# Two cross-attention layers on one core: inputs handed over transposed, x projected in float32, new instruction orders

## The reference

```python
# layer 0
q = x @ Wq + bq; k = ctx @ Wk + bk; v = ctx @ Wv + bv
w = softmax(q @ k.T / 16, axis=queries)        # over the 512 rows of x
x = layernorm(w @ v + x) * gamma + beta
# layer 1
Q = x @ Wq1 + bq1; K = ctx @ Wk1 + bk1; V = ctx @ Wv1 + bv1
out = x + (softmax(Q @ K.T / 16, axis=keys) @ V) @ Wo + bo
```

## Time and profile before

| | us |
|---|---|
| Median of 3 runs (467.13 to 467.44) | 467.43 |
| The profiled execution | 466.4 |
| Its span, first to last instruction | 464.6 |
| Border: `project_q1(0)` starts | 60.4 |
| Borders: `project_q1(1)` to `project_q1(7)` start | 113.7, 167.0, 220.2, 273.6, 327.0, 379.3, 428.2 |

### The profile page before, as it was taken

The page is one execution under the profiler, slowest core; times in us unless marked ns, Lnnn a source line. Parts: engine busy times, 40 slices in busy tenths (PEclk is TensorE's granted clock), DMA queues, the critical chain, the costliest instruction groups (busy, mean ns, idle before and its releaser), DMA issues.

```text
span 464.6 us, 7967 instructions
## 1 busy us (share of the span) xinstructions
PE 443.7 (96%) x2433; PEld 371.6 (80%) x2433; DVE 366.8 (79%) x898; ACT 383.7 (83%) x819; POOL 365.0 (79%) x321
## 2 busy tenths in 40 slices
PE   8798899999999999999999999999999999799796
PEld 8686667887888888888888878888888878687596
DVE  3798978788886988778787888779877887578774
ACT  4899889987999789987899879987899879872473
POOL 0567699979999799887999789987999699963400
PEclk9999999999999999999999999999999999999999
DMA  9400200021100210020200210001100010000001
GB/s 262 130 24 24 71 24 2 23 72 34 36 23 1 72 47 23 24 55 18 70 23 1 71 49 23 24 18 55 46 1 0 3 46 1 0 0 25 23 1 45
DMA packets 23896, 17.29 MB, mean 37 GB/s; under 512 B 1055, under 2 KB 23854, under 8 KB 23854
## 3 DMA queue, kind: packets, MB, share of 16 engines
q1 hardware_dynamic: 23706, 16.66, 11.8%
q10 hardware_dynamic: 148, 0.13, 0.1%
HBM read 12.59 MB, written 4.19 MB: 36 GB/s over the span
## 4 chain that ended last, share of the span: by engine, by line
PE 79%; ACT 8%; DVE 5%; POOL 4%; issue 4%; DVEq 0%; POOLq 0%; ACTq 0%
PE ps_l L654 11%; PE ps_l L655 10%; PE ps_l L656 9%; PE ps_s L800 9%; PE ps_s L654 8%; PE ps_s L656 8%; PE ps_s L655 8%; ACT p L1048 3%; PE ps_s L774 3%; PE ps_s L841 3%; DVE max L1257 2%; POOL wsum L1376 2%; PE ps_l L687 2%; ACT p L1001 2%; PE ps_s L768 2%
## 5 line engine op out<-in xcount | busy, mean ns | idle before, releaser
L1376 POOL TENSOR_TENSOR wsum<-wsum,p 128x512 f32<-128x512 f32 (+1 forms) x88 | 116.3, 1322 | 13.4 <-ACT p L1007 11.8
L1383 POOL TENSOR_TENSOR p_lo<-p,p_hi 128x512 fp32r<-128x512 f32 (+1 forms) x91 | 117.2, 1295 | 2.6 <-ACT p_hi L1015 2.4
L1001 ACT ACTIVATE p<-s_sb,min 128x512 f32<-128x512 f32 (+1 forms) x104 | 75.4, 726 | 7.5 <-DVE min L1171 5.3
L1171 DVE CUSTOM_DVE_ANT_0 s_sb<-ps_l,cb 128x512 f32<-128x512 f32 (+1 forms) x104 | 70.4, 685 | 13.3 <-ACT p L1001 5.5
L1007 ACT ACTIVATE p<-p,r 128x512 f32<-128x512 f32 (+1 forms) x104 | 74.9, 728 | 1.4 <-DVE r L1178 1.3
L1192 DVE TENSOR_TENSOR p1T_lo<-ps_s,p1T_hi 128x512 fp32r<-128x512 f32 (+1 forms) x91 | 60.6, 683 | 14.4 <-ACT p1T_hi L1056 13.9
L1257 DVE TENSOR_REDUCE max<-ps_s 128x1 f32<-128x804 f32 x58 | 57.1, 992 | 10.0 <-PE ps_s L656 8.6
L1056 ACT CAST p1T_hi<-ps_s 128x512 fp32r<-128x512 f32 (+1 forms) x91 | 52.0, 586 | 14.9 <-PE ps_s L800 12.1
L1015 ACT CAST p_hi<-p 128x512 fp32r<-128x512 f32 (+1 forms) x104 | 63.5, 624 | 0.5 <-PE ps_l L656 0.4
L1048 ACT ACTIVATE p<-ps_s,bias 128x1206 f32<-128x1206 f32 (+1 forms) x58 | 53.6, 927 | 3.6 <-DVE bias L1268 3.1
L800 PE MATMUL ps_s<-ident,p 128*128 128x128 f32 (+1 forms) x364 | 49.6, 273 | 1.5 <-ACT p L1048 1.5
(11 more groups left out here) (181 smaller groups left out, 1100.1 us busy)
## 6 DMA issues: line engine op xcount, KB each, us to landing
ctx_sb<-in_ctx_dram SPq DMA_DIRECT2D x24, 256.0 KB, 2.9
x_sb<-in_x_dram SPq DMA_DIRECT2D x8, 512.0 KB, 3.6
out_dram<-y_res SPq DMA_DIRECT2D x16, 256.0 KB, 2.2
p<-in_L_xattn_Wq_dram SPq DMA_DIRECT2D x2, 256.0 KB, 4.2
ctx_sb<-in_ctx_dram SPq DMA_DIRECT2D x8, 32.5 KB
p<-in_L_xattn_Wv_dram SPq DMA_DIRECT2D x2, 128.0 KB, 4.3
p<-in_L_xattn_Wo_dram SPq DMA_DIRECT2D x1, 256.0 KB, 4.7
p<-in_L_xattn_Wk_dram ACTq DMA_DIRECT2D x1, 128.0 KB, 3.3
```

The costliest lines, as they stand in the source:

```text
L1001: nc.scalar.activation(p0[0:m, ring0(i), :], s0_sb[0:m, (a + i) % 2, :], ACT.Exp, bias=min0[0:m, i:i + 1], scale=-1.0, accum_out=sum0[0:m, ...
L1171: nc.vector.tensor_tensor_reduce(out=s0_sb[0:m, (a + i) % 2, :], in0=ps_s0[0:m, (a + i) % 2, :], in1=cb[a % 2][0:m, :], scale=-SCALE, scal ...
L1376: nc.gpsimd.tensor_tensor(total, total, p0[0:m, ring0(i), :], ALU.add).then_inc(wsum_done, 1)
L1383: nc.gpsimd.tensor_tensor(p0_lo[0:m, h, :], p0[0:m, ring0(i), :], p0_hi[0:m, h, :].bitcast(F32), ALU.subtract).then_inc(p0_lo_done, 1)
```

## The change

The host now hands over x and ctx both as they are and transposed, and the weights transposed; bias vectors come as columns. So `turn_x`, `turn_ctx`, `turn_wq`, `turn_wk`, `turn_vectors`, `turn_w1`, `x_turned`, `xT_low` and `repeat` are gone. `project_q0` takes the transposed x directly in two plain float32 products. `ctx_high` and `ctxT_low` read the loaded `ctxT_sb` in SBUF. ctx has one buffer, ctxT one, xT two. In batch 0 the context is split on GpSimd (`ctx_split_first`) and the odd tiles' `p0_high` on VectorE (`p0_high_first`). `residual1` is two instructions. SP's order and all four engines' orders are new.

```diff
         x_sb = [sb(f"x_sb{p}", [P, TB, E]) for p in range(2)]
-        ctx_sb = [sb(f"ctx_sb{p}", [P, MT, L]) for p in range(2)]
+        xT_sb = [sb(f"xT_sb{p}", [P, EC, T]) for p in range(2)]
+        ctx_sb = sb("ctx_sb", [P, MT, L])
+        ctxT_sb = sb("ctxT_sb", [P, M])
         ctx_hi = [sb(f"ctx_hi{p}", [P, MT, L], F32R) for p in range(2)]
...
-        xT_hi, xT_lo = (sb(f"xT_{part}", [P, EC, T], F32R) for part in ("hi", "lo"))
...
+            def load_xT(c):
+                if c >= 2:
+                    sp.wait_ge(qw0_ps, c - 1)
+                sp.dma_start(xT_sb[c % 2][:], xT[bass.ds(c, 1)].rearrange("o (c p) t -> p (o c) t", p=P)
+                             ).then_inc(xT_loaded[c % 2], 16)
+
+            def load_ctxT(c, g):
+                if c >= 1:
+                    sp.wait_ge(ctxT_lo_done, GROUPS * (c - 1) + g + 1)
+                lo, hi = group_cols(g)
+                sp.dma_start(ctxT_sb[:, lo:hi], ctxT[bass.ds(c, 1), :, lo:hi].rearrange("o l m -> (o l) m")
+                             ).then_inc(ctxT_loaded[g], 16)
...
             def load_ctx(c, g):
-
-                if c >= 2:
-                    sp.wait_ge(ctx_lo_done, GROUPS * (c - 2) + g + 1)
-                    sp.wait_ge(pv0_ps, MT * (c - 2) + group(g)[-1] + 1)
+                if c >= 1:
+                    sp.wait_ge(ctx_lo_done, GROUPS * (c - 1) + g + 1)
...
+                sp.dma_start(wqT[0], wq0T.rearrange("(h p) e -> p h e", p=P)).then_inc(w_loaded[0], 16)
+                load_xT(0)
+                load_ctxT(0, 0)
                 load_x(0)
-                for g in range(GROUPS):
+                load_ctx(0, 0)
+                for g in range(1, GROUPS):
+                    load_ctxT(0, g)
                     load_ctx(0, g)
...
+                sp.dma_start(wqT[1], wq1T.rearrange("(h p) e -> p h e", p=P)).then_inc(w_loaded[1], 16)
+                sp.dma_start(wkT[1], wk1T.rearrange("(h p) l -> p h l", p=P)).then_inc(w_loaded[1], 16)
+                sp.dma_start(cols[1][:], cols1).then_inc(cols_loaded[1], 16)
+                load_xT(1)
...
                 load_x(1)
-                for g in range(GROUPS):
-                    load_ctx(1, g)
-                sp.dma_start(wv0_sb, wv0).then_inc(wv_loaded, 16)
-                sp.dma_start(wv1_sb, wv1).then_inc(wv_loaded, 16)
-                sp.dma_start(wo_sb, wo.rearrange("(c p) d -> p c d", p=P)).then_inc(wv_loaded, 16)
+                sp.dma_start(wv0_sb, wv0).then_inc(wv0_loaded, 16)
...
+                sp.dma_start(wvT, wv1T.rearrange("(h p) l -> p h l", p=P)).then_inc(wv_loaded, 16)
+                sp.dma_start(wo_sb, wo.rearrange("(c p) d -> p c d", p=P)).then_inc(wv_loaded, 16)
+                for g in range(GROUPS):
+                    load_ctxT(1, g)
+                for g in range(GROUPS):
+                    load_ctx(1, g)
...
-            for c in range(2, B + 3):
+            for c in range(2, B + 2):
                 if c < B:
+                    load_xT(c)
+                    load_x(c)
+                    for g in range(GROUPS):
+                        load_ctxT(c, g)
                     for g in range(GROUPS):
                         load_ctx(c, g)
-                    load_x(c)
-                if c >= 3:
-                    store(c - 3)
+                store(c - 2)
...
             def project_q0(a, _):
-                pe.wait_ge(xT_lo_done, EC * (a + 1))
+                pe.wait_ge(xT_loaded[a % 2], 16 * (a // 2 + 1))
                 misc_free("project_q0", a)
                 if a == 0:
-                    pe.wait_ge(weights_lo_done, 1)
+                    pe.wait_ge(made_sb, 1)
                 for c in range(EC):
-                    mm = split3(ps_misc[:], a0_hi[:, c, :], a0_lo[:, c, :], xT_hi[:, c, :], xT_lo[:, c, :],
-                                start=(c == 0), stop=(c == EC - 1))
+                    mm = nc.tensor.matmul(ps_misc[:], a0_sb[:, c, :], xT_sb[a % 2][:, c, :], start=(c == 0), stop=(c == EC - 1))
                 mm.then_inc(qw0_ps, 1)
...
+            def weigh_bias(ps, col, w):
+
+                for h in range(EC):
+                    mm = nc.tensor.matmul(ps, col[:, h:h + 1].broadcast_to([P, P]), w[:, h, :], start=(h == 0), stop=(h == EC - 1))
+                return mm
+
+            def make_w0(_, i):
 
                 if i == 0:
...
+                    pe.wait_ge(wk0_loaded, 16)
+                    pe.wait_ge(w_loaded[0], 16)
+                    make_a(0, s1_bank(2)).then_inc(made_ps, 1)
...
+            def make_w1(_, i):
...
+                if i == 0:
...
                     pe.wait_ge(w_loaded[1], 16 * 2)
-                    turn_wq(1, s1_bank(0))
+                    pe.wait_ge(cols_loaded[1], 16)
+                    pe.wait_ge(made_sb, 1)
+                    make_a(1, s1_bank(2))
+                    weigh_bias(s1_bank(2)[:, E:2 * E], bk_col[1], wqT[1]).then_inc(made_ps, 1)
...
             def ctx_high(a, g):
-                act.wait_ge(ctxT_ps, GROUPS * a + g + 1)
+                act.wait_ge(ctxT_loaded[g], 16 * (a + 1))
+                if a >= 2:
+                    act.wait_ge(s1_ps, KC * TB * (a - 1))
                 lo, hi = group_cols(g)
-                nc.scalar.copy(ctxT_hi[a % 2][:, lo:hi], ctx_bank(a, g)[:, 0:hi - lo]).then_inc(ctxT_hi_done, 1)
+                nc.scalar.copy(ctxT_hi[a % 2][:, lo:hi], ctxT_sb[:, lo:hi]).then_inc(ctxT_hi_done, 1)
 
             def ctx_split(a, g):
-                act.wait_ge(ctx_loaded[a % 2][g], 16 * (a // 2 + 1))
+                act.wait_ge(ctx_loaded[g], 16 * (a + 1))
...
                 m = rows(i)
-                nc.scalar.copy(p0_hi[0:m, (MT * a + i) % RH, :], p0[0:m, ring0(i), :]).then_inc(p0_hi_done, 1)
+                nc.scalar.copy(p0_hi[0:m, (MT * a + i) % RH, :], p0[0:m, ring0(i), :]
+                               ).then_inc(p0_hi_even if a == 0 else p0_hi_done, 1)
...
             def ctxT_low(a, g):
                 dve.wait_ge(ctxT_hi_done, GROUPS * a + g + 1)
                 lo, hi = group_cols(g)
-                nc.vector.tensor_tensor(ctxT_lo[a % 2][:, lo:hi], ctx_bank(a, g)[:, 0:hi - lo],
+                nc.vector.tensor_tensor(ctxT_lo[a % 2][:, lo:hi], ctxT_sb[:, lo:hi],
                                         ctxT_hi[a % 2][:, lo:hi].bitcast(F32), ALU.subtract).then_inc(ctxT_lo_done, 1)
...
+            def p0_high_first(a, i):
+
+                dve.wait_ge(norm0_done, i + 1)
+                if (held := split_before(a, i)) is not None:
+                    dve.wait_ge(pv0_ps, held)
+                m = rows(i)
+                nc.vector.tensor_copy(p0_hi[0:m, i % RH, :], p0[0:m, ring0(i), :]).then_inc(p0_hi_odd, 1)
...
+            def ctx_split_first(a, g):
+
+                pool.wait_ge(ctx_loaded[g], 16)
+                m = rows(group(g)[0])
+                tiles = slice(group(g)[0], group(g)[-1] + 1)
+                nc.gpsimd.tensor_copy(ctx_hi[0][0:m, tiles, :], ctx_sb[0:m, tiles, :]).then_inc(ctx_hi_first, 1)
...
                 for h in range(2):
                     pool.wait_ge(out_free[h], 16 * (b + 1))
-                for t in range(TB):
-                    ins = nc.gpsimd.tensor_tensor(y_res[:, t, :], xhat[:, t, :], gamma_row[:], ALU.mult)
-                ins.then_inc(y_part_done, 1)
+                nc.gpsimd.tensor_tensor(y_res[:], xhat[:], gamma_row[:].unsqueeze(1).broadcast_to([P, TB, E]), ALU.mult
+                                        ).then_inc(y_part_done, 1)
                 pool.wait_ge(y_part_done, b + 1)
-                for t in range(TB):
-                    ins = nc.gpsimd.tensor_tensor(y_res[:, t, :], y_res[:, t, :], betaob_row[:], ALU.add)
-                ins.then_inc(y_res_done, 1)
+                nc.gpsimd.tensor_tensor(y_res[:], y_res[:], betaob_row[:].unsqueeze(1).broadcast_to([P, TB, E]), ALU.add
+                                        ).then_inc(y_res_done, 1)
...
+    made = dict(
+        x=inputs["x"], xT=np.asarray(inputs["x"]).transpose(0, 2, 1),
+        ctx=inputs["ctx_512"], ctxT=np.asarray(inputs["ctx_512"]).transpose(0, 2, 1),
+        wq0T=w["L0Wq"].T, wk0T=w["L0Wk"].T, cols0=columns(w["L0bq"], w["L0bk"]), wv0=w["L0Wv"], bv0=w["L0bv"],
+        gamma=w["L0gamma"], beta=w["L0beta"],
+        wq1T=w["L1Wq"].T, wk1T=w["L1Wk"].T,
+        cols1=columns(w["L1bq"], w["L1bk"], w["L1bv"], w["L0gamma"], w["L0beta"]),
+        wv1T=w["L1Wv"].T, wo=w["L1Wo"], bo=w["L1bo"])
```

346 lines of the change are left out of this document (113 added, 233 removed), and 464 rows, old and new, of tables (GPSIMD_HEAD, GPSIMD_STEADY, SCALAR_HEAD, SCALAR_STEADY).

## The result

| | before | after |
|---|---|---|
| Median, with lowest and highest of 20 runs (us) | 467.08 (466.09 to 468.73) | 469.34 (468.15 to 478.5) |
| Ratio, 95% interval | | 1.0063 [1.0036, 1.0089] |
| The profiled execution | 466.4 | 474.97 |
| Its span | 464.6 | 473.1 |
| `project_q1(0)` starts | 60.4 | 63.57 |

What follows compares the result with a forecast made beforehand. TensorE was taken to bound the steady part, ScalarE the head. 466.4 less 10.3 (steady part), 1.3 (start) and 0.8 (rest of batch 0) gave 454.0; 1.0 to the median made 455.0, put at 454.5 us, range 449.5 to 461.5.

Steps and rivals of the forecast that it cites:

- The steady part: Later batches: TensorE loses turns, so the period falls from 53.3 to 51.5 us; 10.3 us saved over the intervals.
- The twin of L774: In `project_q0`: six products of 0.23 us (1.39) become two float32 products in L774's form, 1.72 us.
- the added 0.3 of waits: Steady part: 0.3 us more waits per interval for the fuller engines, added by choice; bounds -0.5 and +2.0.
- The fourth rival: Turns are hidden and cost nothing; only the dearer product and the head's 2.1 us remain, 467.3 us; chance 0.03.
- the price of `ctxT_low`: VectorE's two-SBUF-input instruction beside GpSimd: costs GpSimd about 0.4 us, itself 0.1 in the mean, 0.45 at worst.
- The third rival: Each large `ctxT_low` holds GpSimd for its whole 0.69 us; 54.4 us a batch, 471.9 us in all; chance 0.05.
- VectorE has room in the head: Batch 0: VectorE gains 1.1 us of work, but idle time falls from 4.1 to 2.2 us; 0.8 us shorter.
- GpSimd's 93%: Steady part: GpSimd stays at 47.7 us busy, now in some 51.5 us, 93% where it was 89%.
- The clock: TensorE's granted clock, read as 1.00 in the steady part of the earlier profile.

Runs made afterwards that it cites:

- the meeting kernel: The kernel after, with GpSimd waiting ahead of 23 steps of batches 1 to 7 until the `ctxT_low` there is done; 467.68 us, ratio 0.9996.
- Experiment 1: Separate 233 us kernel without the computation: VectorE starts one instruction inside the second of six GpSimd additions; with two SBUF inputs, 1.0 us of standing.
- experiment 8: The meeting kernel with 52 useless 128x128 products at six places of TensorE's head: 468.06 us; with odd casts also back on ScalarE, 467.53 us.
- 7: The meeting kernel with batch 0's odd-tile `p0_high` casts back on ScalarE and `p0_high_first` gone; 467.86 us, ratio 1.001.
- 9: The meeting kernel with `scores0(1, 6)` moved ahead of `turn_y(0)` in TensorE's order; 471.47 us, ratio 1.0095.
- 11: The meeting kernel with batch 1's `p0_low` moved to VectorE: tiles 0 and 1, 470.78 us; tiles 0, 1, 4, 6 and 8, 475.75 us.
- 12: The meeting kernel with `ctx_low(1, 0)` and `sum_weights(1, 1)` ahead of `p0_low(1, 0)` on GpSimd: 471.25 us; with four more head waits 473.85 us.
- 4: The run that made the meeting kernel: the kernel after plus GpSimd's 23 waits for `ctxT_low`; 467.68 us, ratio 0.9996.
- 5: The kernel after with `residual1` in eight instructions again; 471.34 us, ratio 1.0068.
- 6: The kernel before with only `residual1` changed, to two instructions of 1024 elements; 467.6 us, ratio 1.0004.
- 13: The kernel after with the orders of the kernel before, without the removed steps; 492.02 us, ratio 1.0486.
- 10: The meeting kernel with GpSimd's `sum_weights` cut to 32 of 512 columns: batch 0, 465.54 us; batch 1, 464.2 us; both, 463.12 us.

## Why the prediction was wrong, step by step

**The steady part was right, except for its last interval.** 51.75 us against 51.5, in the meeting kernel for three intervals, with 52.2 ahead of them. The twin of L774 in `project_q0` has the form forecast (four instructions in 1.88 to 1.96, as L774's own, 1.88 to 1.98); GpSimd busy 47.2 to 47.8 where 47.7 was forecast, ScalarE 46 (46.7), the DMA queue 18.2% (19%), no waits of ScalarE for DMA but 3.5 us at the start. `max0(0, 0)` started at 14.44 (forecast 14.0, before 15.35). But the sum counted six such intervals, and the sixth is 52.5 in the meeting kernel (52.3 before, 50.6 forecast), the seventh 49.3 (48.7). In the sixth TensorE's weight loads waited 3.1 us for layer 1's exponentials, 0.6 before. These 2.4 us are another miss of the added 0.3 of waits; no experiment touched them. The fourth rival (the turns cost nothing) gave 467.3, close to what was measured, but its mechanism is refuted by the 51.75; that the total came out near it is chance.

**The step that failed: the price of `ctxT_low` and of the two-input and cast steps around it.** From the earlier trace rows the prediction made "0.1 in the mean, 0.45 at worst" for VectorE, and 0.4 for GpSimd. That row shows a VectorE instruction that stood only 0.45 us, because little of GpSimd's instruction was left. Experiment 1 shows what the row can't: VectorE waits for GpSimd's whole running instruction, 1.0 us of standing with 65 columns as with 512, and GpSimd loses under 0.3. I put the loss on the wrong engine. The third rival has the right mechanism the wrong way round: it lets GpSimd lose the time in every batch, and the steady 51.75 us show that it doesn't. Instead there were single stands of 3.4 and 5.75 us, which TensorE waited out and then worked at half clock. In after they cost 2.3 us up to the third border (174.55 against 172.2) and 5.8 in the fifth batch.

**The second failed step: VectorE has room in the head.** I gave it 2.2 us of idle time between `max0(0, 0)` and the border. It had 4.7 in after and 4.5 in the meeting kernel, with 44.6 us busy, about 6 of these being stands behind GpSimd. The earlier trace rows showed 41.5 of 46.2, and the sum added 1.1: an engine so full can't also carry waits. With most of the stands gone (sums of batches 0 and 1 cut) `predict(0, 0)` came 2.85 us earlier, but the border only 0.9; see the account below.

**The third: GpSimd's 93% was an average.** The earlier trace rows has 47.7 of 53.3 for a later batch. In the second stage before it had 49.82 of 53.3. The stretch by itself wasn't read. In the meeting kernel it is 51.1 of 56.6.

**The clock** was taken as 1.00 throughout, since it was so before. It is 0.93 in the first stage and 0.94 in the second. Every fall in the stretches of 2 us follows a pause of TensorE, though not every pause brings one (at 60 to 62 us TensorE was busy for 0.44 of 2, at 1.00). Work taken off TensorE makes pauses where another engine is the bound. After a single stand of 3 us its half-speed products lie behind one another, and in the head they make the way from `predict(0, 0)` to `predict(0, 1)` 3.7 us instead of 2.2 (experiment 8).

**The account to the third border** (forecast 60.4 - 2.1 + 2 x 51.6 = 161.5): after 174.55; the long stand 2.3; the sums of batches 0 and 1 in GpSimd's queue, and what VectorE stands for them, 3.7 (172.2 to 168.5); rest 7.0. (Behind it the meeting kernel adds 0.3 in three intervals, 2.4 in the last two, and the end is 0.6 shorter: 12.8 us over the 454.0 of the sum.) For the rest the starts in the first stage (us) help:

| start of | before | after | meeting kernel | sums of batches 0, 1 cut |
|---|---|---|---|---|
| `predict(0, 0)` | 51.47 | 53.26 | 53.06 | 50.21 |
| `predict(0, 1)` | 53.30 | 56.99 | 56.78 | 54.19 |
| `turn_y(0, 0)` | 58.55 | 61.56 | 61.35 | 59.38 |
| `project_q1(0)` | 60.4 | 63.57 | 63.37 | 62.43 |

With the sums cut, batch 0 reaches `predict` 1.3 us earlier than before (2.1 forecast), and then loses 2.1 between the two predicts, where after puts two `scores0` of batch 1 at half clock (2.6 us, 1.4 at full) in the place of a 0.9 us wait, and it loses 1.2 between `turn_y` and the border. That is 4.1 us short of the forecast in the first stage; the second (54.1 against 51.6) and the third give the rest. Experiments 7, 8, 9, 11 and 12 didn't bring it back. That the half clock is part of it follows from experiment 8's trace: at 1.00 the two `predict` start 2.2 us apart, in the version with both sums cut 4.0. The 1.2 us are of the same kind: the eight turns of `turn_y` take 1.97 us there and 1.09 before. Together that is up to 3.0 of the 4.1 us, an estimate from these rows that no version tried by itself. An order that puts the two `scores0` ahead of `predict(0, 0)` again, where before has them and after has a pause of 1.7 us, wasn't tried.

**What is shown and what isn't.** Shown: the kind of instruction that stands and for how long (1); that long stands make all of the loss against before (4), and that `residual1` doesn't (5, 6); that going back to the old orders doesn't mend it (13); that GpSimd's load in batch 1 holds the second stage by 2.6 us (10). Not settled: why VectorE misses several borders in a kernel and none in a bare row; how the first stage's last 4 us divide between the half clock (by estimate 0.6 to 1.9 in the meeting kernel, up to 3.0 with the sums cut), the new place of the two `scores0` and the rest; and the 2.4 us of the last two intervals. No version tried that computes the whole is faster than before by more than can be measured.

## What to carry to other kernels

When data moves from PSUM to SBUF, ask not only what the copy or turn cost but what kind of instruction its reader becomes: beside a GpSimd that is 90% busy, a VectorE instruction with two SBUF inputs costs its own time plus up to the rest of GpSimd's running instruction, and at times several of them. Price such a step by the longest of its kind in a busy stretch, not by its mean, and if TensorE reads its result, give it a place where GpSimd can be made to wait. Read every stage's fullest engine by itself before an average lets you take time off TensorE.

## What the runs showed of the hardware

- A held VectorE instruction shows as a longer instruction, not as idle time: 65 columns took 0.23, 1.20 or 5.75 us. Busy shares hide the stall.
- A VectorE instruction with one SBUF input and two columns stands like one with two inputs (1.40), and so does `scalar_tensor_tensor` (1.39); a reduction doesn't (0.69).
- The hold is lopsided between streams: VectorE stood through five GpSimd instructions (5.75 us), while a GpSimd addition among seven VectorE instructions took 1.26 to 1.55.
- TensorE fell from 2.4 to 1.2 GHz (granted 0.73 in 90 to 92 us, 0.50 in 92 to 96) in a stand of 3.1 us, and its 512-column products went from 0.23 to 0.43 us apart.
- Products put in to keep the clock up aren't free: 14 float32 products of 128x128 held TensorE for 3.05 us, 0.22 each, and the step behind them began 1.4 us after its input was there.
